# A fused decoder layer on one core: 64-key softmaxes normalised through the exponent, landmark softmax formed transposed

## The reference, cut to what matters

```python
x = x + attn(_layernorm(x), Wqkv, bqkv, Wout, bout)           # 16 heads of 16
x = x + xattn(_layernorm(x), ctx, ctx, mask, Wq, ..., Wo, bo)  # keys: 64 context rows
x = x + ffn(_layernorm(x), ...)                                # one of 8 experts per batch entry

# attn: 64 landmarks, each the mean of 8 tokens
sim1 = q @ k_l.T          # 512 x 64 per head
sim2 = q_l @ k_l.T        # 64 x 64
sim3 = q_l @ k.T          # 64 x 512
attn1, attn2, attn3 = softmax(sim1), softmax(sim2), softmax(sim3)
V = attn2
for _ in range(6):        # pseudo-inverse of attn2
    KV = attn2 @ V
    V = 0.25 * V @ (13 * I - KV @ (15 * I - KV @ (7 * I - KV)))
out = (attn1 @ (V @ (attn3 @ v))) @ Wout + bout

# xattn: scores Q @ K.T / 4, masked keys set to -1e9, softmax over 64 keys, @ V, @ Wo.T + bo
```

## Time and profile before

| | us |
|---|---|
| runs | 1507.07, 1519.60, 1503.67; median 1507.07 |
| profiled execution | 1512.32, its span 1510.3 |
| PE busy | 1435.8 |
| DVE busy | 1014.2 |
| ACT busy | 744.4 |
| POOL busy | 569.5 |
| mean granted clock of PE | 0.983 of full speed |

### The profile page before, as it was taken

How to read it: one execution, slowest core, us unless ns; L and a number is a source line. 1 busy time by engine, 2 the same in 40 slices (tenths; PEclk the granted TensorE clock), 3 DMA queues, 4 the chain that set the end, 5 groups by cost and what they waited for, 6 DMA issues and landing times.

```text
span 1510.3 us, 51059 instructions
## 1 busy us (share of the span) xinstructions
PE 1435.8 (95%) x22484; PEld 947.6 (63%) x22484; DVE 1014.2 (67%) x2098; ACT 744.4 (49%) x1434; POOL 569.5 (38%) x688
## 2 busy tenths in 40 slices
PE   8989999999999999999999999999999999997765
PEld 6756566666757666676766666675665667565433
DVE  1667767767676777767677776767677676767440
ACT  2425554645555563655556364455645445563321
...
DMA packets 40270, 53.02 MB, mean 35 GB/s; under 512 B 9442, under 2 KB 30194, under 8 KB 40050
## 3 DMA queue, kind: packets, MB, share of 16 engines
...
## 4 chain that ended last, share of the span: by engine, by line
PE 89%; issue 6%; DVE 2%; POOL 2%; ACT 1%; POOLq 1%; DMA 0%; SPq 0%; DVEq 0%; ACTq 0%
PE bank L1051 41%; PE bank L1069 7%; PE bank L1276 7%; PE bank L1079 6%; PE bank L1263 4%; PE bank L1163 3%; PE bank L1122 3%; PE bank L1231 2%; PE bank L1143 2%; PE bank L1172 2%; PE bank L1059 2%; PE bank L1244 2%; PE bank L1149 1%; PE bank L1222 1%; PE bank L1157 1%
## 5 line engine op out<-in xcount | busy, mean ns | idle before, releaser
L543 POOL TENSOR_TENSOR b<-ut,eye 128x256 f32<-128x256 f32 x192 | 136.8, 731 | 361.3 <-DVE ut L896 341.7
L701 ACT ACTIVATE az<-bank 128x320 f32<-128x320 f32 x192 | 66.7, 399 | 200.5 <-PE bank L1069 200.0
L1051 PE MATMUL bank<-xnT_c,w1e 128*128 128x512 f32 x256 | 129.5, 632 | 8.8 <-DMA row_e<-w2o_row 8.8
L952 DVE RECIPROCAL oT_x<-bank 128x256 f32<-128x256 f32 x64 | 107.7, 1724 | 35.2 <-PE bank L1276 35.2
L649 ACT ACTIVATE p<-bank,nm 128x512 f32<-128x512 f32 x128 | 87.0, 688 | 83.2 <-DVE nm L841 83.0
L1051 PE MATMUL bank<-xnT_a,wqkv 128*128 128x512 f32 x256 | 125.5, 614 | 0.0
L1051 PE MATMUL bank<-w2e,hT 128*128 128x256 f32 x512 | 118.8, 385 | 2.7 <-ACT hT L756 2.7
L719 ACT ACTIVATE pT<-bank 128x512 f32<-128x512 f32 x128 | 69.5, 604 | 104.8 <-PE bank L1265 104.7
L952 DVE RECIPROCAL oT<-bank 128x256 f32<-128x256 f32 x64 | 112.4, 1756 | 6.8 <-PE bank L1276 4.3
L926 DVE TENSOR_REDUCE m<-bank 128x8 f32<-128x512 f32 x128 | 82.2, 684 | 46.4 <-PE bank L1231 46.4
L447 POOL TENSOR_SCALAR var_eps_c<-mv_c 128x4 f32<-128x4 f32 x16 | 3.7, 234 | 283.0 <-DVE mv_c L777 283.0
...
## 6 DMA issues: line engine op xcount, KB each, us to landing
...
```

What stands on the lines that cost most here:

```text
L543: return g.tensor_tensor(b7[:, q, :], ut[:, q, :], eye[28 if it else 7][:].unsqueeze(1) .broadcast_to([P, 4, LM]), ALU.subtract).then_inc( ...
L952: return v.reciprocal(oT[x][:, k, half], tile(i, ("den" + x, k))[:, half]).then_inc(dve_done, 1)
L1051: last = mm(dst, lhsT, rhs, start=(k == 0), stop=(k == len(pairs) - 1))
```

## The change

The two softmaxes over 64 keys get their sums another way. After the maximum, DVE subtracts it from the score tile into `ee` (`sb`), ACT takes the exponential in place (`en`), POOL adds halves of rows, 64 to 32 to 16 to 8 values (`sm`), DVE the rest (`es`), and ACT takes the logarithm (`ln`). `mp` adds it to the maximum before the cut into parts, so that the transposed scores come out with maximum and logarithm subtracted, and their exponential is normalised. `den`, `rec` and the multiplication go; `o1`, `ox` become copies on ACT.

For sim3 the maxima are cut and transposed like the others (`mp3`, `mT3`), and `t3` forms the scores with keys on partitions, so that the exponential writes `p3T` directly. The sums come from columns of ones beside v (`vt` has 16 values and 16 ones for each head); `zT` works head by head with 64 columns, and `z` divides by the sum that arrives beside it. The transposes `p3T` go, `s3` stays for the maxima.

The second layer norm's rows are formed on ACT (`nmB`) and no longer on POOL. x is read a second time into `x1` (SP step `x1`), where `xr` adds the bias. A batch entry with all keys masked is handled in the mask. `TURN` is a new table for all steps, with at most 5 turns between an entry's start and its end in the place of 12 (the first nine of which held none of its steps).

```diff
 TURN = """
-    S.fc A.az.4.0-11 D.lmq.0-10 A.az.4.1-11 A.e1.1.2-11 P.den1.0-11 D.wb.4.0-11 D.wb.4.1-11 D.lmq.1-10
...
+    S.fc G.sm1.1.0-3 P.o1.0-4 D.logit-5 G.sm1.1.1-3 D.soft2-3 A.o1.0-4 D.mx1.1.2-3 D.mx1.1.3-3 D.fb-2
...
@@ emptied_by
-            return ({"e3": "s3", "e1": "t1", "ex": "tx"}[kind], n[0]), (n[1],)
+            return ({"e3": "t3", "e1": "t1", "ex": "tx"}[kind], n[0]), (n[1],)
...
-        if kind in ("mx1", "mxx"):
+        if kind in ("mx3", "sb1", "sbx"):
             return ("s" + kind[-1], n[0]), (n[1],)
@@ SP
+                elif kind == "x1":
+                    if c := unmet(sp, "D", i - 1, ("wx", 0), ("wx", 1)):
+                        sp.wait_ge(dve_done, c)
+                    sp.dma_start(x1[:], x_dram[:, i * T:(i + 1) * T, :]).then_inc(x1_loaded, 16)
@@ POOL
+                if kind in ("sm1", "smx"):
...
+                    e = ee[x][:, j % 2]
+                    for w in (32, 16):
+                        g.tensor_tensor(e[:, :, :, 0:w], e[:, :, :, 0:w], e[:, :, :, w:2 * w], ALU.add)
+                        g.drain()
+                    return g.tensor_tensor(e8[x][:, :, j, 2 * k:2 * k + 2, :], e[:, :, :, 0:8], e[:, :, :, 8:16],
+                                           ALU.add).then_inc(pool_done, 1)
                 if kind == "lnB":
...
-                    return normalise("b", x1).then_inc(pool_done, 1)
+                    g.tensor_tensor(shift_b[:], mv["b"][:, :, 0], rstd["b"][:], ALU.mult)
+                    g.drain()
+                    return g.tensor_scalar(shift_b[:], shift_b[:], -1.0, None, ALU.mult).then_inc(pool_done, 1)
@@ ACT
-                    return s.activation(p3[:, j], tile(i, ("s3", k), j)[:], ACT.Exp, bias=nm3[:, c:c + 1],
-                                        accum_out=sum3[:, c:c + 1]).then_inc(act_done, 1)
-                if kind == "p3T":
...
-                    return s.activation(p3T[:, n % 4], tile(i, step)[:].rearrange("p (t c) -> p t c", t=T),
-                                        ACT.Copy).then_inc(act_done, 1)
+                    return s.activation(p3T[:, j].rearrange("p t c -> p (t c)"), tile(i, ("t3", k), j)[:],
+                                        ACT.Exp).then_inc(act_done, 1)
+                if kind in ("en1", "enx"):
...
+                    e = ee[x][:, j % 2].rearrange("p t h c -> p (t h c)")
+                    return s.activation(e, e, ACT.Exp).then_inc(act_done, 1)
+                if kind in ("ln1", "lnx"):
...
+                    return s.activation(esum_ln[x][:].rearrange("p t j c -> p (t j c)"),
+                                        esum[x][:].rearrange("p t j c -> p (t j c)"), ACT.Ln).then_inc(act_done, 1)
+                if kind in ("o1", "ox"):
...
+                    return s.activation(oT[x][:, n, :], tile(i, step)[:], ACT.Copy).then_inc(act_done, 1)
+                if kind == "nmB":
...
+                    for t in range(T):
+                        last = s.activation(xn["b"][:, t, :], x1[:, t, :], ACT.Identity, bias=shift_b[:, t:t + 1],
+                                            scale=rstd["b"][:, t:t + 1])
@@ DVE
+                if kind in ("sb1", "sbx"):
...
+                    n = 4 * k + j - 2
+                    if n >= 0:
+                        if c := unmet(dve, "G", i, ("sm" + x, n // 4, n % 4)):
+                            dve.wait_ge(pool_done, c)
...
+                    return v.tensor_tensor(ee[x][:, j % 2], tile(i, ("s" + x, k), j)[:].rearrange(
+                        "p (t h c) -> p t h c", t=T, h=2), m[x][:, :, j, 2 * k:2 * k + 2].unsqueeze(3)
+                        .broadcast_to([P, T, 2, LM]), ALU.subtract).then_inc(dve_done, 1)
+                if kind in ("es1", "esx"):
...
+                    return v.tensor_reduce(esum[x][:].rearrange("p t j c -> p (t j c)"),
+                                           e8[x][:].rearrange("p t j c e -> p (t j c) e"), AX.X, ALU.add).then_inc(dve_done, 1)
                 if kind in ("mp1", "mpx"):
...
+                    v.tensor_tensor(m[x][:], m[x][:], esum_ln[x][:], ALU.add)
+                    v.drain()
...
-                if kind in ("rec1", "recx"):
...
-                    return v.reciprocal(oT[x][:, k, half], tile(i, ("den" + x, k))[:, half]).then_inc(dve_done, 1)
@@ PE
-                elif kind == "p3T":
...
-                        last = nc.tensor.transpose(o[:, t * P:(t + 1) * P], p3[:, n % 4, t * P:(t + 1) * P], ident[:])
+                elif kind == "mT3":
...
+                    for k in range(KD):
+                        last = mm(o[:, k * P:(k + 1) * P], m3_parts[:, k].rearrange("p j c -> p (j c)"), ident_bf[:],
+                                  start=True, stop=True)
+                elif kind == "t3":
...
+                    for j in range(4):
+                        mm(tile(i, step, j)[:], minus3[rows(j), :], m3T[rows(j), n, :].unsqueeze(1)
+                           .broadcast_to([32, T, P]), start=True, stop=False)
+                    for t in range(T):
+                        for j in range(4):
+                            last = mm(tile(i, step, j)[:, t * P:(t + 1) * P], kT[rows(j), n, t * P:(t + 1) * P],
+                                      flat(qbd[rows(j), n]), start=False, stop=(t == T - 1))
                 elif kind == "zT":
...
-                            last = mm(o[rows(j), 0:P], vt[:, t, c:c + 2 * DH], p3T[:, j, t, :],
-                                      start=(t == 0), stop=(t == T - 1))
+                    for h in range(2):
+                        q = slice(LM * h, LM * h + LM)
+                        for t in range(T):
+                            for j in range(4):
+                                last = mm(o[rows(j), q], vt[:, t, 2 * (4 * n + j) + h, :], p3T[:, j, t, q],
+                                          start=(t == 0), stop=(t == T - 1))
-                elif kind in ("den1", "denx", "o1", "ox"):
+                elif kind in ("o1", "ox"):
```

306 lines of the change are left out of this document (174 added, 132 removed).

## The result

The changed kernel takes 1516.55 us (median of 20 runs, 1508.45 to 1527.83) against 1507.39 for the kernel before: ratio 1.0061, 95% interval 1.0039 to 1.0083. The forecast was 1480, with a range up to 1508: 27 us less, where it came out 9 more. The profiled execution takes 1515.42 us with a span of 1513.6; that of the kernel before, from which the forecast was worked out, was 1512.32 with 1510.3. So 30 of the 36.5 us that are missing can be read from the two profiles (a span of 1483 was forecast), and 6 are the place of a profiled execution among its runs: 5 us over the median before, 1 under it now.

The account below looks back on a forecast made before the run. TensorE was taken to bound the kernel: 4.1 us less work an entry less 1.95 of waits is 2.15, 34 for 16 entries; with 7 for the ends, 1512-34+7=1485 for the profile, 1480 for the median, range 1440 to 1508.

Parts of the forecast that it names:

- TensorE's net work: TensorE per batch entry: 7.6 us removed less 3.5 added, 4.1 us less, 66 in all.
- The transposed scores: Two added TensorE steps forming the landmark scores transposed: 2.7 us an entry together, 1.35 each.
- the product with v: TensorE, 64 instructions of half the width for 32: 1.3 us a step, +0.6 for both, between 0 and 2.0.
- the better end of the net: TensorE's net with every price at its better end, 5.4 us an entry; the forecast's own range then starts at 1462.
- (a): Third layer norm: VectorE's statistics and copies of iteration 4 take 5.4 us, TensorE has 4.2 and waits 1.2 an entry.
- (b): First cross scores wait for a bank that ACT must copy out first: 0.45 us an entry.
- (c): Cross attention softmax: TensorE's banks follow POOL; 0.3 us an entry, with a small wait at the turn's start.
- Both are hidden as totals: DVE at some 60 us and ACT at about 55 an entry, in a turn of 83, were taken to cost nothing.
- at the full granted clock: Earlier profile, 300 to 1300 us: PE busy 990 of 1000 us at 2.4 GHz.
- The ends: First and last turns, where nothing covers a chain: cross attention 4.7 us longer, first turns some 2; 7 added.
- more stretches like (a): Rival: banks used harder, 1.2 us more an entry, 19 lost again, 1499 for the profile; chance 0.2.
- POOL ends the turn: Rival: POOL's sums at 2.3 us a tile make the entry 89.1 us, 48 more in all, 1555; chance 0.08.

Follow-up runs that it names:

- the sixth experiment: The first experiment with the third layer norm's statistics split, two tiles taken before VectorE waits for the projection's other half: 1490.0 us, ratio 0.9885.
- the ninth experiment: The first experiment with VectorE's sum wx.0 put ahead of ScalarE's copy az.4.1, so iT.4 gets other banks: 1495.5 us, ratio 0.9917.
- the fifth experiment: The first experiment with two of GpSimd's three additions per tile left out, so only 16 of 64 keys are summed: 1485.49 us, ratio 0.9854.
- The first experiment: The changed kernel with GpSimd's base and row made to wait for VectorE's mp3 of the entry two further: 1498.21 us, ratio 0.9935.
- the fifteenth run: Sums' chain on 8 of 64 keys, against a kernel with the first experiment's wait, exchanged banks, split statistics and xnTa.1 between iT.4 and jT.4: 1465.28 us.
- the other pair: The fifteenth run and the kernel it was made from, which has the chain on all 64 keys: 1465.28 and 1477.79 us.

## Why the prediction was wrong, point by point

**TensorE's net work: right.** The short turn less its waits (0.96, 0.60, 0.49, 0.2, 0.16) is 82.2 us; a turn before, less its 0.5, was 86.2. That is 4.0 against the 4.1 forecast. That it comes so near is in part luck, since two terms were off and cancel. The transposed scores take 1.22 us each (1.35 forecast), and the product with v costs nothing more:

```profile
752.01 0.39 PE L1246 MATMUL bank<-m3T,minus 32*128 32x512 bf16 x4
752.24 1.06 PE L1250 MATMUL bank<-qbd,kT 32*128 32x128 f32 x32
753.23 1.10 PE L1261 MATMUL bank<-p3T,vt 128*32 128x64 f32 x64
...
760.89 1.10 PE L1261 MATMUL bank<-p3T,vt 128*32 128x64 f32 x64
761.92 1.98 PE L1122 MATMUL bank<-xnT_a,wqkv 128*128 128x512 f32 x4
```

64 instructions in 1.03 us, 16 ns each; the earlier trace rows had 1.02 for 32 of twice the columns, so columns bound it. The floor of the Trainium skill, "TensorE: Matmul & The Clock Gate" (Part 1), some 25 ns an instruction, would give 1.6 us; this trace does not have it. The added steps come to 2.6 us by these rows, where I had 3.5, which leaves 6.6 us for what was removed, where I took 7.6, if nothing else changed on TensorE; which of the two steps is smaller was not measured apart. (A slip of the range: 21 us less for the better end of the net make 1459, not 1462.)

**(a), the third layer norm: near in size, wrong in cause.** Forecast 1.2 us; it is 0.60 + 0.96. The statistics are through in time (the sixth experiment ends them at 700.95, 1.2 us before `wb` begins, and both waits stay); it is a bank that comes back one step too late (the ninth experiment takes the 0.60 away) and a chain of TensorE, VectorE, TensorE with no filler. I added up durations and did not look whose bank `iT.4` gets.

**(b): right. (c): right in size only.** For (b) it is 0.49 for 0.45, at the first cross scores and for zT. For (c) it is 0.20 and 0.16 for 0.3, but the Newton step behind the transposed maxima and the landmark scores, which were to wait, do not: the 0.20 stand ahead of the second half of the transposed cross scores, the 0.16 ahead of the product `uz`, `attn2T` behind the last iteration. GpSimd's pieces came a little dearer than the line through two rows of before gave:

```profile
L561 POOL TENSOR_TENSOR ee_x<-ee_x 128x256 f32<-128x256 f32 x128 | 93.0, 727 | 85.5 <-ACT ee_x L717 85.5
...
L561 POOL TENSOR_TENSOR ee_x<-ee_x 128x128 f32<-128x128 f32 x128 | 58.9, 460 | 18.8 <-issue 0.9
...
L563 POOL TENSOR_TENSOR e<-ee 128x64 f32<-128x64 f32 x128 | 41.3, 323 | 18.2
```

0.73, 0.46 (0.51 in the first attention) and 0.32 where I had 0.73, 0.40, 0.24: 1.74 us a tile against 1.67. It hurt nothing in the turns, as the fifth experiment shows.

**What failed: two costs of the turn that the sum had at nothing.** The turn without them is there, 84.5 to 84.9 us in six of the first 13. Against 84.6 for each, these 13 come out 32 us over, 1131.9 for 1099.8; the forecast gets 24 of these wrong, since the kernel before has 9 us of longer turns of its own (1136.3 for 13 times 86.7) that it carried along. The first experiment gets 21 of the 32 back, and the 11 that it leaves are, to a microsecond, ten turns with one drop of the clock, 1.2 us each.

The first cost is the block of VectorE's small steps by GpSimd. The step of the prediction is "Both are hidden as totals": I listed durations and totals of the engines, and walked the order for (a) to (c), but never laid the new order of GpSimd beside the new order of VectorE. In the kernel before these steps stood beside a long piece of GpSimd too, in nearly every turn, but at its end:

```profile
584.54 2.37 POOL L465 TENSOR_TENSOR x<-x,box_row 128x1024 f32<-128x1024 f32 x1
...
586.84 0.18 DVE L937 CAST m_parts<-m 128x64 bf16<-128x64 f32 x1
```

There the cast begins 0.07 us before the piece ends, and the steps took their 0.2 us. In the changed kernel they lie just ahead of `base` and `row`, and a small delay puts them behind: a step of 0.2 us then costs 2.4. The second cost is that delay, the lowered clock. The forecast took the turn "at the full granted clock" of the earlier trace rows over to the new order, no rival had another, and what sets the early drop off these runs did not find.

**The ends: 8 us too short in sum, and wrong in place.** What lies outside the 15 turns was 210 us and is 223 (226 in the first experiment), where the forecast had 215. But the forecast had the chain of the cross attention at the end, 4.7 us, and 2 us for the start. In the changed kernel the first output projection comes at 179.2 us for 162.4, 17 us later. By windows TensorE runs 2577 matmul instructions ahead of it for 2136 and is busy 8 us more, so half of it is work that the new table does earlier; the other half is idle time, 22.5 us for 14.1, with new or longer waits of 0.6 to 3.3 us for `m_parts`, `m_parts_x`, `kbd`, `uz` and `m3T`. The last two turns take 158.6 for 163.9 and what follows 43.8 for 47.8: 9 us less, where the forecast, with three shares of 2.15 us off and 4.7 on, had 2 less. So of the 30 us that are missing in the span the start has 15 and the turns 24, and the end gives 8 back. The chain of the sums costs 8 to 9 us in the last two turns by the fifth and the fifteenth run, and next to nothing at the start (first projection at 181.5 for 182.6 in the fifth, 181.8 in both of the other pair). What the start's waits are worth no experiment tested. The lower clock has a share, too: the earlier trace rows and the windows after it give 0.91 and 0.86 for the last stretch, 0.98 and 0.97 for the first.

Of the rivals, "more stretches like (a)" gave the nearest time, by another mechanism. "POOL ends the turn" is excluded by the fifth run: GpSimd's sums at 0.32 us a tile instead of 1.74 leave the first 13 turns at the same 1111.2 us.
